# Layer-1 experts with two accumulators in DRAM in place of four, and each scatter-add waiting for the one before it

## The reference, cut to what matters

```python
def moe(x, router_w, w_gate, w_up, w_down, ws_gate_up, ws_down):   # E=64 experts, top K=8, C=64 slots each
    probs = softmax(x @ router_w.T)
    topk_w, topk_ids = top_k(probs, 8);  topk_w /= topk_w.sum(-1, keepdims=True)
    # the first 64 tokens (in token order) that chose an expert get a slot of it, later ones are dropped
    xb = gather(x, slots)                                   # (64 experts, 64 slots, 128)
    y  = einsum(silu(xb @ w_gate) * (xb @ w_up), w_down)    # hidden width 96
    routed = segment_sum(y[slot] * topk_w, token)           # every token sums its experts
    gu = x @ ws_gate_up
    shared = silu(gu[:, :96]) * gu[:, 96:] @ ws_down
    return routed + shared
```

## Time and profile before

| what | value |
|---|---|
| median of 3 runs | 2866.97 us (2863.68 to 2868.86) |
| the profiled execution's own time | 2868.79 us |
| its span, first to last instruction | 2867.1 us |
| mean granted TensorE clock | 0.859 of full speed |
| PE busy | 2200.6 us (77%) |
| DVE busy | 1743.5 us (61%) |
| POOL busy | 832.6 us (29%) |
| line 1267, scatters of the layer-1 experts | x64, 101.7 us busy, 1588 ns each |
| first `l1_ffn`, from its first SP instruction to its last statistics | 585.0 to 787.2 us |
| second `l1_ffn` | 869.6 to 1071.0 us |

### The profile page before, as it was taken

The page is one execution under the profiler, slowest core; times in us unless marked ns, Lnnn a source line. Parts: engine busy times, 40 slices in busy tenths (PEclk is TensorE's granted clock), DMA queues, the critical chain, the costliest instruction groups (busy, mean ns, idle before and its releaser), DMA issues. The chain is left out here.

```text
span 2867.1 us, 45613 instructions
## 1 busy us (share of the span) xinstructions
PE 2200.6 (77%) x13241; PEld 1646.1 (57%) x13242; DVE 1743.5 (61%) x4336; ACT 1074.8 (37%) x2668; POOL 832.6 (29%) x757
## 2 busy tenths in 40 slices
PE   4988968967376732475999941775999899989999
PEld 3874547847364730364455521664888555547877
DVE  5556965663477348851366668824556677855555
ACT  1653316641044101253444412452333266663332
POOL 2544525437413741375100010773000122200000
PEclk9998969975597556798999975997999899999999
DMA  4110001166605667256222264563000323310000
GB/s 156 38 56 11 1 32 39 36 217 130 177 5 186 134 176 145 58 117 138 61 61 59 60 156 65 111 120 85 1 0 0 85 62 88 93 35 5 7 7 12
DMA packets 283973, 216.96 MB, mean 76 GB/s; under 512 B 103140, under 2 KB 254481, under 8 KB 280753
## 3 DMA queue, kind: packets, MB, share of 16 engines
q1 hardware_dynamic: 249648, 181.06, 23.4%
q0 software_dynamic: 34176, 34.09, 7.3%
HBM read 148.95 MB, written 65.17 MB: 75 GB/s over the span
## 5 line engine op out<-in xcount | busy, mean ns | idle before, releaser
L162 POOL TENSOR_TENSOR fields<-ln_t,power 128x4 f32<-128x4 f32 x96 | 98.3, 1055 | 374.0 <-DVE ln_t L155 373.9
L3368 DVE TENSOR_REDUCE s_mx<-s_sa 128x2 f32<-128x512 f32 x256 | 166.0, 686 | 48.4 <-PE s_sa L3518 47.0
L3448 ACT ACTIVATE s_e<-s_sc 128x512 f32<-128x512 f32 x256 | 149.2, 600 | 93.5 <-PE s_sc L3537 90.7
L3114 PE MATMUL s_z<-s_t,s_mix_h 128*128 128x256 f32 x768 | 171.3, 379 | 0.0
L2019 POOL DMA_INDIRECT acc_dram<-s_yo,s_to_i x96 | 152.4, 1588 | 45.3 <-issue 28.3
L2007 POOL DMA_INDIRECT s_xg<-rows_dram,s_from_i x96 | 94.5, 984 | 222.7 <-DVE s_to_i L2140 194.7
L3114 PEld LDWEIGHTS s_z<-s_t,s_mix_h 128*128 128x128 f32 x768 | 145.8, 190 | 20.6 <-issue 1.0
L2324 PE MATMUL s_hu<-s_xgt,s_w 128*128 128x128 f32 x768 | 117.1, 298 | 7.5 <-issue 6.1
L191 PE MATMUL s_tp<-ident,xn 128*128 128x128 f32 x192 | 39.8, 344 | 107.6 <-DVE xn L181 106.0
L573 DVE SCALAR_TENSOR_TENSOR s_hs<-s_ha,s_b,s_sg 128x128 f32<-128x128 f32 x312 | 87.9, 345 | 52.6 <-ACT s_sg L627 25.2
L3164 PE MATMUL s_z<-xnt,s_wt_w 128*128 128x512 f32 x256 | 118.0, 616 | 1.5 <-ACT xnt L197 1.5
(11 more groups left out here) (548 smaller groups left out, 5923.9 us busy)
## 6 DMA issues: line engine op xcount, KB each, us to landing
s_w<-in_L_ffn_W_dram SPq DMA_DIRECT2D x96, 256.0 KB
s_share<-share_dram SPq DMA_DIRECT2D x32, 512.0 KB, 6.0
acc_dram<-s_zero SPq DMA_DIRECT2D x24, 512.0 KB, 6.1
acc_dram<-fields SPq DMA_DIRECT2D x4, 2048.0 KB, 11.5
fields<-acc_dram SPq DMA_DIRECT2D x16, 512.0 KB, 5.9
table_dram<-s_table_rows SPq DMA_DIRECT2D x2, 3136.0 KB, 10.0
s_wg<-in_L_ffn_w_gate_dram SPq DMA_DIRECT2D x64, 96.0 KB
s_wu<-in_L_ffn_w_up_dram SPq DMA_DIRECT2D x64, 96.0 KB
```

What stands on the lines that cost most here:

```text
L162: pool.tensor_tensor(core.rstd[:, tiles], core.ln_t[:, 2, tiles], core.power[:, 0:CT], ALU.pow).then_inc(s.scale_ready.sem, 1)
L3114: last = pe.matmul(bank(n)[:, o, :], weights[:, f, o * P:(o + 1) * P], src[:, f, :], start=f == 0, stop=f == HALF - 1)
L3368: dve.tensor_reduce(mx[:, i, t, 2 * pairs:2 * pairs + 2], sa[:, n % 2, :, :], AX.X, ALU.max).then_inc(max_done.sem, 1)
L3448: act.activation(e[:, n % RING, :, :], sc[:, n % 2, :, :], ACT.Exp).then_inc(exp_done.sem, 1)
```

## The change

The number of accumulator regions goes from four to two. Region 2 and 3 are no longer zeroed, loaded back or added. The index list `to_i` is made by one instruction with one offset for all n. The scatter of step n now waits for scatter n - 1, since consecutive scatters add to the same two regions. The wait stands where the old one stood, behind the gather of the same step.

```diff
-        region = s.sb("region", [P, 2])
+        region = s.sb("region", [P, 1])
...
-        acc = [core.x, core.all_xn, table_rows[:, :, 0:D], xnt[:, :, :].rearrange("p c (t d) -> p (c t) d", d=D)]
+        acc = [core.x, core.all_xn]
...
             sp.dma_start(region_rows(0), core.x[:, :, :]).then_inc(zeroed.sem, 16)
-            for b in range(2, 4):
-                for n in range(TILES // 8):
-                    sp.dma_start(region_rows(b)[:, n * 8:(n + 1) * 8, :], zero[:, :, :]).then_inc(zeroed.sem, 16)
-            for b in range(4):
+            for b in range(2):
                 sp.dma_start(sums[b * ROWS + TOKENS:(b + 1) * ROWS, :], zero[0:CAP, 0, :]).then_inc(zeroed.sem, 16)
...
             for q in range(4):
                 tiles = slice(q * 8, (q + 1) * 8)
-                for b in range(4):
+                for b in range(2):
                     sp.dma_start(acc[b][:, tiles, :], region_rows(b)[:, tiles, :]).then_inc(acc_loaded[q].sem, 16)
...
-            pool.wait_ge(zeroed.sem, 16 * (2 * TILES // 8 + 5 + 1))
+            pool.wait_ge(zeroed.sem, 16 * (1 + 2 + 1))
...
-                if n > 1:
-                    pool.wait_ge(added[n % 2].sem, 16 * (n // 2))
+                if n > 0:
+                    pool.wait_ge(added[(n - 1) % 2].sem, 16 * ((n + 1) // 2))
                 pool.indirect_dma_start(sums, bass.IndirectOffsetOnAxis(ap=to_i[:, n:n + 1], axis=0),
                                         yo[:, n % RING, :], None, compute_op=ALU.add).then_inc(added[n % 2].sem, 16)
...
-                dve.tensor_scalar(region[:, 1:2], upper[:, :], float(ROWS), float(2 * ROWS), ALU.mult, ALU.add)
...
-            pairs = lambda t: t[:, :].rearrange("p (n u) -> p u n", u=2)
-            dve.tensor_scalar(pairs(to_i)[:, 0, :], pairs(row)[:, 0, :], region[:, 0:1], None, ALU.add)
-            dve.tensor_scalar(pairs(to_i)[:, 1, :], pairs(row)[:, 1, :], region[:, 1:2], None, ALU.add).then_inc(index_ready.sem, 1)
+            dve.tensor_scalar(to_i[:, :], row[:, :], region[:, 0:1], None, ALU.add).then_inc(index_ready.sem, 1)
...
             for q in range(4):
-                dve.wait_ge(acc_loaded[q].sem, 64)
+                dve.wait_ge(acc_loaded[q].sem, 32)
                 c8 = slice(q * 8, (q + 1) * 8)
                 dve.tensor_tensor(core.x[:, c8, :], core.x[:, c8, :], acc[1][:, c8, :], ALU.add)
-                dve.tensor_tensor(acc[2][:, c8, :], acc[2][:, c8, :], acc[3][:, c8, :], ALU.add)
-                dve.drain()
-                dve.tensor_tensor(core.x[:, c8, :], core.x[:, c8, :], acc[2][:, c8, :], ALU.add)
                 dve.drain()
```

## The result

| | before | after |
|---|---|---|
| median of 18 runs each, taken side by side | 2867.52 us | 2877.20 us |
| ratio, with its 95% interval | | 1.0039 (1.0025 to 1.0053) |
| first layer-1 stage, its first SP transfer to the next stage's | 203.2 us | 208.3 us |
| second layer-1 stage, the same | 202.3 us | 207.0 us |
| the profiled execution's time (span) | 2868.79 (2867.1) | 2891.51 (2889.8) |

The change costs 9.7 us by the medians (their quotient is 1.0034, inside the interval); 2876 was forecast, with +9.2 as its sum. In the two profiled executions the stages grew by 5.1 and 4.7 us, 9.8 in all, which is as much as the medians differ by.

The account below looks back on a forecast made before the run. POOL's issuing was taken to bound the layer-1 loop at 3.18 us a step. Terms 11.5 + 8.0 - 14.8 - 0.1 = +4.6 us a stage, +9.2 in all, took 2866.97 to 2876 us; range 2863 to 2890.

Parts of the forecast that it names:

- steps 3 to 27: Layer-1 loop over pairs: each step 3.64 us instead of 3.18, 11.5 us lost a stage over twenty-five steps.
- last four steps: Loop's end, no gather, both waits ahead of the scatter: 4 x 4.02 = 16.1 us instead of 8.1, 8.0 lost a stage.
- reload, additions, statistics: Stage's end, first reload to last statistics: 17.44 us, as in the layer-2 expert stage, instead of 32.27; 14.8 less.
- zeroing and list: Stage's front: removed zero stores gain nothing; DVE's index list loses one instruction, 0.1 us gained a stage.
- Landing and answer: Loop step: 3.37 us from scatter start to SP's reload at stage end, plus POOL's 0.27 us start after a wait.
- The two answers: POOL's delay after release: 0.27 us behind one wait, 0.75 behind two; the loop's scatter was given 0.27.
- The cover: Stage's front: DVE's list releases POOL's first gather after 8.30 us idle, hiding the zero stores; their removal counted as nothing.
- The hidden landing: Rival, loop: landing hides behind the gather, step 3.46 us or less; at 3.3, -6.8 us a stage, 2853; chance 0.12.
- The late answer: Rival, loop: every step costs 4.02 us like the last ones, +14.1 us a stage, 2895; chance 0.16.

Follow-up runs that it names:

- run with the mended order: Changed kernel, last four steps only: the wait for the previous scatter put ahead of the wait for `yo`; scatters 27 to 31 took 14.38 and 14.27 us; one execution 2885.12 us.
- run with the loads kept: Kernel before without the two additions of regions 2 and 3, all sixteen loads kept; the stage's end took 30.2 and 29.4 us.
- run with two waits: Changed kernel with a second wait, for `yo`, ahead of every step's wait for the previous scatter; 4.09 and 4.10 us a step, one execution 2911.85 us.
- run with the wait alone: Kernel before with four regions, zeroing and reload kept, but scatter n waits for scatter n - 1; ratio 1.0128, +38.9 us.

## Why the prediction was right, point by point

| term, per stage | predicted | first | second |
|---|---|---|---|
| steps 3 to 27 | +11.5 | +11.6 | +11.3 |
| last four steps | +8.0 | +8.0 | +8.1 |
| reload, additions, statistics | -14.8 | -14.6 | -15.1 |
| zeroing and list | -0.1 | +0.4 | 0.0 |
| the rest of the stage | 0 | -0.3 | +0.3 |
| sum | +4.6 | +5.1 | +4.7 |

In before, scatters 2 to 27 take 79.6 us in either stage and 27 to 31 take 8.1; the ends are those of the earlier trace rows, and the first gather comes 59.4 and 59.1 us behind the stage's first transfer. The after side is the timeline above, where the first gather comes 641.89 - 582.10 = 59.8 and 59.1 us behind it.

*What bounds the loop.* POOL's issuing did until the change, a landing does now. Prediction 3.64 us a step, measured 3.65 and 3.64, with the one late landing of 4.77 in the first. The window of the earlier trace rows shows it from the other side: DMA share down from 0.70 to 0.63, PE from 63.07 to 55.06 us busy.

*Landing and answer.* The sum of 3.37 + 0.27 was taken from two places that had nothing to do with a step of the loop, and as a sum it held; no run measures its two parts one by one. That it came out to the hundredth is partly luck. SP's own answer is in the 3.37, and the prediction set it against the loop's traffic. The run with the mended order shows that traffic to be worth little: its last four steps, with the engines nearly empty, take 3.59 and 3.57 us a step, its loop 3.62 and 3.60. So the sum is some 0.06 too long where nothing disturbs, traffic adds about 0.03, and the late landing of 4.77 adds 0.05 to the first stage's mean. The two answers, 0.27 and 0.75, differ by 0.48, and that difference is confirmed from both sides: taking it out of the last steps gave 0.46 a step, putting it into the loop cost 0.45.

*The last steps.* 4 x 4.02 was right because before already showed dependent pairs there. The prediction did not see that the order of the two waits, not their number, decides it.

*The end.* 17.44 was borrowed from the layer-2 stage; measured 17.78 and 17.09. The run with the loads kept adds that the transfers bound the end of before, and the rows of after that DVE bounds its end now.

*Zeroing.* The cover was named, and putting the stores back cost nothing that the traces show. The 0.1 us counted for the shorter list did not appear; the front of the stage is 0.4 and 0.0 us longer.

*The rivals.* The hidden landing (3.46 or less) did not come: no pair of scatters from 2 to 27 in after stands closer than 3.47. The late answer did not come either, but it is real, as the run with two waits shows. The prediction had let a figure of the Trainium skill weigh for it: DMA: Bandwidth & Descriptors, Anatomy of one DMA, gives a fixed cost of about 2.0 us plus the bytes over 436 GB/s for each DMA, an estimate of 2.15 us for a scatter's 64 KB. The prediction put that behind the issue and came to 4.01; but that page of the Trainium skill counts setup as well as completion in its fixed cost, so the issue's 1.59 us should not have been added in full. From the start of a scatter the run with the mended order has 3.58 - 0.27 = 3.31 us to the landing, 1.2 more than the sum of 2.15; behind the issue it has 3.31 - 1.55 = 1.76, 0.4 less. The measurement decides: by neither count does the 2.15 give this step, and that 4.01 fell on the late answer's 4.02 was chance. The rule of the Trainium skill, same page, Rules for kernel authors, to wait for a DMA late, held: a wait brought one scatter forward cost 18 to 19 us a stage in the run with the wait alone.

## What to carry to other kernels

A wait for a transfer is free only as long as its landing plus the waiter's answer is shorter than the work the queue does anyway; here 3.64 against 3.18. The 0.46 us a step over 25 steps and the last four steps' 8.0 us outweighed an end that was nearly halved. Price such a wait from a place in the old trace that already has it (the ends of loops, where nothing covers a landing), and write the wait that ends last ahead of one that is over already. Before pricing half of a transfer at half of its time, look how far behind it the engine is that uses it. Read a term's worth from the stage it lies in: the whole program's time moved by up to 19 us more or less than its edited stages.

## What the runs showed that I had not expected

The order of two waits ahead of one DMA is worth 0.46 us: 4.04 a step with the late one second, 3.58 with it first.

Eight loads of 512 KB issued beside three dependent scatters of 64 KB stretched the distances from 3.6 us to 3.9, 8.2 and 5.8. The Trainium skill, DMA: Bandwidth & Descriptors, section Queues, rings and completion order, has each engine take turns between the queues packet by packet. The trace neither bears this out nor rules it out: scatter 29 landed ahead of the last early loads, as scatter 30 starts at 754.97 and DVE's last early addition follows its loads at 760.28; but scatter 31, which waits for 30, starts behind that, at 760.76.

Cutting the four regions' end into half parts brought only 1.0 us a stage, since DVE needs more for two halves (2 x 3.0 us) than for a whole (5.3).

Layer 3 took between 884 and 905 us in fourteen profiles of the same instructions there, with a granted clock of 0.97 down to 0.95.
